# Gate and up products of the experts in halves instead of fp32, with the weights split once per tile

## What is computed

```
x = x + state_space_and_self_attention(layernorm(x))
x = x + cross_attention(layernorm(x), ctx)
x = x + experts(layernorm(x))              # the stage of the change
x = x + attention(layernorm(x)); x = x + cross(layernorm(x), ctx); x = x + int8_product(layernorm(x))
```

```
down_e( silu(z @ gate_e) * (z @ up_e) )    # gate_e, up_e: 256 x 512, down_e: 512 x 256, all fp32
```

## Time and profile before

| | us |
|---|---|
| three runs | 1214.91, 1215.37, 1217.53 (median 1215.37) |
| profiled execution, its own time | 1215.94 |
| its span (first to last instruction of the core) | 1214.1 |
| PE busy in the span | 1151.8 (95%) |
| DVE, ACT, POOL busy | 793.4 (65%), 719.0 (59%), 711.1 (59%) |
| TensorE's granted clock, mean over the span | 0.99 of full |
| costliest PE group: gate and up (L1736), 312 records | 146.7 |
| down (L1753), 312 records | 73.9 |

### The profile page before, as it was taken

How to read it: one execution, slowest core, us unless ns; L and a number is a source line. 1 busy time by engine, 2 the same in 40 slices (tenths; PEclk the granted TensorE clock), 3 DMA queues, 4 the chain that set the end, 5 groups by cost and what they waited for, 6 DMA issues and landing times.

```text
span 1214.1 us, 23112 instructions
## 1 busy us (share of the span) xinstructions
PE 1151.8 (95%) x7745; PEld 924.9 (76%) x7745; DVE 793.4 (65%) x1835; ACT 719.0 (59%) x2084; POOL 711.1 (59%) x783
## 2 busy tenths in 40 slices
PE   8999999999989999999989899988999999998996
PEld 7888888888877888888877677768566666667875
DVE  6788888889855566676676688767332333315796
ACT  6778787878724555555554788870223443225873
POOL 5799889898741234242354777750467556633664
PEclk9999999999999999999999899999999999999999
DMA  7000000000020000000030142610622222321001
GB/s 280 1 19 32 19 31 18 30 18 17 2 67 5 1 1 1 1 1 1 2 96 10 62 157 90 251 36 23 162 45 44 44 45 45 51 39 58 1 27 44
DMA packets 40373, 56.98 MB, mean 47 GB/s; under 512 B 8432, under 2 KB 35056, under 8 KB 38608
## 3 DMA queue, kind: packets, MB, share of 16 engines
q1 hardware_dynamic: 31536, 45.43, 11.2%
q0 software_dynamic: 8736, 10.25, 5.4%
HBM read 43.93 MB, written 11.74 MB: 46 GB/s over the span
## 4 chain that ended last, share of the span: by engine, by line
PE 45%; issue 7%; DVE 7%; ACT 6%; POOL 4%; DMA 1%; POOLq 0%; ACTq 0%; DVEq 0%
PE bank L1736 11%; PE bank L1753 5%; PE bank L44 4%; PE bank L46 3%; PE bank L45 3%; ACT x_prob L1390 3%; PE bank L847 2%; PE bank L875 2%; PE bank L858 2%; PE bank L1500 2%; PE bank L1484 1%; PE bank L1745 1%; PE bank L1430 1%; PE bank L2226 1%; POOL a_prob L1019 1%
## 5 line engine op out<-in xcount | busy, mean ns | idle before, releaser
L510 DVE SCALAR_TENSOR_TENSOR ssm_conv<-bank,conv_w,ssm_conv 128x508 f32<-128x508 f32 (+2 forms) x240 | 160.6, 733 | 14.2 <-ACT ssm_conv L400 14.2
L911 ACT ACTIVATE a_prob<-a_prob,a_neg_max 128x128 f32<-128x128 f32 x256 | 99.7, 391 | 116.6 <-DVE a_neg_max L957 116.6
L1019 POOL TENSOR_TENSOR a_prob<-a_prob,a_inv 128x512 f32<-128x512 f32 x64 | 66.6, 1041 | 138.9 <-DVE a_inv L962 138.9
L1736 PE MATMUL bank<-expert_raw,x_kept_next_t 128*128 x312 | 146.7, 593 | 1.2 <-ACT x_kept_next_t L1816 1.2
L674 POOL TENSOR_TENSOR ssm_u_lo<-ssm_conv,ssm_u_hi 128x512 fp32r<-128x512 f32 x80 | 101.4, 1292 | 25.2 <-ACT ssm_conv L410 25.2
L1678 POOL DMA_INDIRECT x_rows<-e_y,e_index x39 | 63.0, 1616 | 73.8 <-ACT e_y L1844 69.5
L44 PE MATMUL bank<-w_out_hi,ssm_u_hi 128*128 128x256 f32 x320 | 92.7, 290 | 3.4 <-POOL ssm_u_lo L674 3.4
L1960 DVE COPY e_h_t<-bank 128x512 f32<-128x512 f32 x39 | 27.0, 692 | 105.3 <-PE bank L1745 102.1
L1390 ACT ACTIVATE x_prob<-bank,x_neg_max 128x128 f32<-128x128 f32 x256 | 89.7, 399 | 7.2 <-DVE x_neg_max L1367 7.2
L46 PE MATMUL bank<-w_out_hi,ssm_u_lo 128*128 128x256 f32 x320 | 91.0, 284 | 0.0
L45 PE MATMUL bank<-w_out_lo,ssm_u_hi 128*128 128x256 f32 x320 | 90.9, 284 | 0.0
(11 more groups left out here) (359 smaller groups left out, 3330.7 us busy)
## 6 DMA issues: line engine op xcount, KB each, us to landing
expert_raw<-in_experts_laid SPq DMA_DIRECT2D x8, 1536.0 KB, 7.8
attn_raw<-in_attn_w_laid SPq DMA_DIRECT2D x1, 4096.0 KB, 18.0
w_in_raw<-in_L_attn_in_proj_w SPq DMA_DIRECT2D x5, 640.0 KB, 5.7
w_out_raw<-in_L_attn_out_proj_w SPq DMA_DIRECT2D x5, 512.0 KB, 4.0
x_res<-in_x SPq DMA_DIRECT2D x4, 512.0 KB, 5.6
x_res<-in_x SPq DMA_DIRECT2D x1, 2048.0 KB, 8.8
x_context<-in_ctx_t_laid SPq DMA_DIRECT2D x8, 256.0 KB, 3.7
z_rows<-x_kept_next_z SPq DMA_DIRECT2D x8, 256.0 KB, 2.2
```

The source lines that it names most:

```text
L510: op = dve.scalar_tensor_tensor(out=acc, in0=xs, scalar=conv_w[:, c, TAPS - 1 - back:TAPS - back], in1=acc, op0=ALU.mult, op1=ALU.add)
L911: e = act.activation(prob[:, m % 4, i, :], prob[:, m % 4, i, :], ACT.Exp, bias=neg_max[:, m % 4, i:i + 1], accum_out=total[:, m % 4, i:i + 1])
L1019: pool.tensor_tensor(prob[:, t % 4, :, :], prob[:, t % 4, :, :], inv[:, t % 4, :].unsqueeze(2).broadcast_to([P, 4, P]), ALU.mult).then_inc ...
L1736: mm = pe.matmul(bank[:, :], rows_t[:, t % 2, k, :], W[:, bass.ds(at + (column + k * FFN), FFN)], start=(k == 0), stop=(k == KD - 1))
```

## The change

Gate and up are computed as products of halves. Per tile, ACT copies the tile's expert's gate and up weights (four pieces of 128 x 512) into high halves `w_hi`, and DVE subtracts to get `w_lo`. There is one buffer each for gate and for up, so a piece is written for t + 1 only after that product of tile t is done. The turned rows are split too (`rows_hi` by ACT, `rows_lo` by DVE, from PSUM). ACT and DVE now read the expert's column into registers of their own. The copy of turned h moves from DVE to ACT in passes 1 to 8 and in the even context tiles. The copy of the turned context by ACT is a function of its own, behind the up half of the split. `w_hi` and `w_lo` lie where `x_res` is, which is in DRAM by then; `gains` and `scaled` move to other addresses. Down is unchanged.

```diff
+    h_on_act = lambda t: 1 <= t <= SEQS // 2 or (turns_context(t) and t % 2 == 0)
...
         def turn_rows(t):
             pe.wait_ge(gathered[t % 3], 16 * (t // 3) + 16)
             if t >= 1:
-                pe.wait_ge(zt_copied, t)
+                pe.wait_ge(rows_split, t)
...
-        def widen(t, at, column, bank, ready):
+        def widen(t, i, bank, ready):
             for k in range(KD):
-                mm = pe.matmul(bank[:, :], rows_t[:, t % 2, k, :], W[:, bass.ds(at + (column + k * FFN), FFN)],
-                               start=(k == 0), stop=(k == KD - 1))
+                pe.wait_ge(w_split[i], t * KD + k + 1)
+                mm = product(pe, bank[:, :], [x[:, t % 2, k, :] for x in (rows_hi, rows_lo)],
+                             [x[:, i, k, :] for x in (w_hi, w_lo)], k == 0, k == KD - 1)
             mm.then_inc(ready, 1)
...
-                pe.wait_ge(zt_copied, t + 1)
+                pe.wait_ge(rows_split, t + 1)
...
+        def split_high(t, at, i):
+            if t >= 1:
+                act.wait_ge((gate_ready, up_ready)[i], t)
+            for k in range(KD):
+                act.activation(w_hi[:, i, k, :], W[:, bass.ds(at + ((GATE_AT, UP_AT)[i] + k * FFN), FFN)],
+                               ACT.Copy).then_inc(hi_ready[i], 1)
...
+        act.wait_ge(x_stored, 16 * PAIRS)
+        act.wait_ge(weights_at_ready, 1)
+        at = offset(act, 0)
...
+        for i in range(2):
+            split_high(0, at, i)
         copy_rows(0)
         for t in range(SLOT_TILES + 1):
+            more = t + 1 < SLOT_TILES
+            if more:
+                at = offset(act, t + 1)
+            if t == 0:
+                split_high(1, at, 0)
             if t < SLOT_TILES:
                 silu(t)
-            if t + 1 < SLOT_TILES:
+            if t >= 1 and h_on_act(t):
+                copy_h(t - 1)
+            if more:
+                if t > 0:
+                    split_high(t + 1, at, 0)
                 copy_rows(t + 1)
+                split_high(t + 1, at, 1)
+                copy_keys(t + 1)
             if t >= 1:
                 copy_y(t - 1)
...
+        def split_low(t, at, i, k):
+            dve.wait_ge(hi_ready[i], t * KD + k + 1)
+            dve.tensor_tensor(w_lo[:, i, k, :], W[:, bass.ds(at + ((GATE_AT, UP_AT)[i] + k * FFN), FFN)],
+                              w_hi[:, i, k, :].bitcast(F32), ALU.subtract).then_inc(w_split[i], 1)
+
+        def rows_low(t):
+            dve.wait_ge(zt_copied, t + 1)
+            dve.tensor_tensor(rows_lo[:, t % 2, :, :], ZT.rearrange("p (k t) -> p k t", k=KD),
+                              rows_hi[:, t % 2, :, :].bitcast(F32), ALU.subtract).then_inc(rows_split, 1)
...
+        dve.wait_ge(weights_at_ready, 1)
+        at = offset(dve, 0)
+        for i in range(2):
+            for k in range(KD):
+                split_low(0, at, i, k)
+        rows_low(0)
         for t in range(SLOT_TILES + 1):
-            if t >= 1:
+            more = t + 1 < SLOT_TILES
+            if t >= 1 and not h_on_act(t):
                 copy_h(t - 1)
+            if more:
+                at = offset(dve, t + 1)
+                split_low(t + 1, at, 0, 0)
+            if t == 0:
+                rows_low(1)
             if t < SLOT_TILES:
                 fuse(t)
+            if more:
+                if t > 0:
+                    rows_low(t + 1)
+                split_low(t + 1, at, 0, 1)
+                for k in range(KD):
+                    split_low(t + 1, at, 1, k)
...
+        with nc.sbuf_tensor("e_w_hi", [P, 2, KD, FFN], F32R) as w_hi, nc.sbuf_tensor("e_w_lo", [P, 2, KD, FFN], F32R) as w_lo:
+            mem["wide_w"] = (w_hi, w_lo)
         mem["x"] = sb("x_res", [P, SEQS, D])
```

More of the change, by code:

```diff
@@ L1141, in stage_cross_attention @@
     for name, shape, dt in KEPT:
+        if name == "next_t":
+            with nc.sbuf_tensor("e_rows_hi", [P, 2, KD, P], F32R) as rows_hi:
+                kept["rows_hi"] = rows_hi
         kept[name] = sb(high, "kept_" + name, shape, dt)
@@ L1592, in stage_experts @@
     rows = sb("rows", [P, 3, D])
-    rows_t = kept["next_t"].rearrange("p a (b t) -> p a b t", t=P)
+    rows_hi, rows_lo = kept["rows_hi"], mem["rows_lo"]
+    w_hi, w_lo = mem["wide_w"]
     gate, h = sb("gate", [P, 2, FFN]), sb("h", [P, 2, FFN])
@@ L1621, in stage_experts @@
     y_sent = [sem(f"y_sent{i}") for i in range(3)]
-    zt_ready, zt_copied = sem("zt_ready"), sem("zt_copied")
+    zt_ready, zt_copied, rows_split = sem("zt_ready"), sem("zt_copied"), sem("rows_split")
+    hi_ready, w_split = (tuple(sem(f"{name}{i}") for i in range(2)) for name in ("hi_ready", "w_split"))
     gate_ready, up_ready, silu_ready, h_ready = sem("gate_ready"), sem("up_ready"), sem("silu_ready"), sem("h_ready")
@@ L1635, in stage_experts, with offset, turned_h @@
     turns_context = lambda t: C_TURN <= t < C_TURN + SEQS
+    h_on_act = lambda t: 1 <= t <= SEQS // 2 or (turns_context(t) and t % 2 == 0)
+    def offset(engine, t):
+        return engine.value_load(weights_at[0:1, t:t + 1], min_val=0, max_val=(EXPERTS - 1) * EXPERT_COLS)
+    def turned_h(t):
+        return HT[t % 2][:, :].rearrange("p (f t) -> p f t", f=KF)
     def sync(sp):
@@ L1755, in down @@
             mm.then_inc(down_ready, 1)
-        offset = lambda t: pe.value_load(weights_at[0:1, t:t + 1], min_val=0, max_val=(EXPERTS - 1) * EXPERT_COLS)
         pe.wait_ge(weights_at_ready, 1)
-        ahead = offset(0)
+        ahead = offset(pe, 0)
         turn_rows(0)
@@ L1765, in tensor @@
                 here = ahead
-                pe.wait_ge(zt_copied, t + 1)
+                pe.wait_ge(rows_split, t + 1)
                 if t >= 2:
                     pe.wait_ge(silu_ready, t - 1)
-                widen(t, here, GATE_AT, GATE[t % 2], gate_ready)
+                widen(t, 0, GATE[t % 2], gate_ready)
             if t >= 1:
@@ L1774, in tensor @@
                     pe.wait_ge(h_ready, t - 1)
-                widen(t, here, UP_AT, UP[t % 2], up_ready)
+                widen(t, 1, UP[t % 2], up_ready)
             if t + 1 < SLOT_TILES:
@@ L1781, in tensor @@
             if t + 1 < SLOT_TILES:
-                ahead = offset(t + 1)
+                ahead = offset(pe, t + 1)
         QK, FT, SCALES = GATE[(SLOT_TILES - 2) % 2], UP[(SLOT_TILES - 2) % 2], HT[(SLOT_TILES - 2) % 2]
@@ L1815, in copy_rows, with copy_keys @@
                 act.wait_ge(up_ready, t - 1)
-            act.activation(rows_t[:, t % 2, :, :], ZT.rearrange("p (k t) -> p k t", k=KD), ACT.Copy).then_inc(zt_copied, 1)
+            act.activation(rows_hi[:, t % 2, :, :], ZT.rearrange("p (k t) -> p k t", k=KD), ACT.Copy).then_inc(zt_copied, 1)
+        def copy_keys(t):
             if turns_context(t):
+                act.wait_ge(rows_split, t + 1)
                 b = t - C_TURN
@@ L1837, in silu, with copy_h @@
             act.activation(gate[:, t % 2, :], GATE[t % 2][:, :], ACT.Silu).then_inc(silu_ready, 1)
+        def split_high(t, at, i):
[4 more added lines that the diff above has]
+                               ACT.Copy).then_inc(hi_ready[i], 1)
+        def copy_h(t):
+            act.wait_ge(ht_ready, t + 1)
+            if t >= 2:
+                act.wait_ge(down_ready, t - 1)
+            act.activation(h_t[:, t % 2, :, :], turned_h(t), ACT.Copy).then_inc(ht_copied, 1)
         def copy_y(t):
@@ L1844, in copy_y @@
             act.activation(y[:, t % 3, :], Y, ACT.Copy, scale=weight[:, t:t + 1]).then_inc(y_copied, 1)
+        act.wait_ge(x_stored, 16 * PAIRS)
+        act.wait_ge(weights_at_ready, 1)
+        at = offset(act, 0)
+        for e in range(EXPERTS):
+            act.wait_ge(mem["expert_loaded"][e], 16)
+        for i in range(2):
+            split_high(0, at, i)
         copy_rows(0)
         for t in range(SLOT_TILES + 1):
+            more = t + 1 < SLOT_TILES
[3 more added lines that the diff above has]
+                split_high(1, at, 0)
             if t < SLOT_TILES:
                 silu(t)
-            if t + 1 < SLOT_TILES:
+            if t >= 1 and h_on_act(t):
[3 more added lines that the diff above has]
+                    split_high(t + 1, at, 0)
                 copy_rows(t + 1)
+                split_high(t + 1, at, 1)
+                copy_keys(t + 1)
             if t >= 1:
@@ L1959, in copy_h @@
                 dve.wait_ge(down_ready, t - 1)
-            dve.tensor_copy(h_t[:, t % 2, :, :], HT[t % 2][:, :].rearrange("p (f t) -> p f t", f=KF)).then_inc(ht_copied, 1)
+            dve.tensor_copy(h_t[:, t % 2, :, :], turned_h(t)).then_inc(ht_copied, 1)
+        def split_low(t, at, i, k):
[6 more added lines that the diff above has]
+                              rows_hi[:, t % 2, :, :].bitcast(F32), ALU.subtract).then_inc(rows_split, 1)
         def fuse(t):
@@ L2460, in decoder @@
         mem["neg_one"] = sb("neg_one", [P, SEQS])
+        mem["gains"], mem["scaled"] = sb("gains", [P, 4, KD]), sb("scaled", [P, 2, KD])
         spare_rows = (SEQS + 1) * P
@@ L2574, in decoder @@
```

(4 more changed lines are left out.)

## The result

| | us |
|---|---|
| after, median of 4 runs | 1195.68 (1195.39 to 1197.90) |
| before, median of 4 runs | 1216.05 (1214.91 to 1217.53) |
| ratio after to before | 0.9833, 95% interval 0.9822 to 0.9845 |
| profiled execution, its span | 1193.7 (before 1214.1) |
| busy: PE, DVE, ACT, POOL | 1128.4, 890.5, 805.1, 729.3 |

The gain is 20.4 us in the medians and in the spans. I forecast 25.2, and a time of 1190.2; the measured one lies in the range.

A forecast was written before the change was run, and what follows sets the result against it. PE was taken to bound the kernel: 36 periods each 0.71 us shorter (25.6), plus 0.71 for tile 38, less 1.05 at the start, give 25.2 us. That made 1190.2 against the runs' median, range 1187.5 to 1201.

The forecast's parts named there:

- PE is the bound and stays it: Expert stage: only PE's work sets the pace, busy all 70.00 us of a stretch, and 99% or more after.
- Twelve products at 0.228: Gate and up per tile: 2.73 us instead of 3.44, saving 0.71; periods 5.11, and 5.32 with context.
- ACT and DVE keep the pace, by 0.13 us: Splits for the next tile: added copies and subtractions finish before PE wants them, by 0.13 us at the tightest place.
- Rival 1: Missed split handshakes before PE's products: up to 0.26 us per tile, time 1193 to 1200; chance 22%.
- The start: 1.05 us lost: Head of the expert stage: first splits and ACT's order move gate(2) from 861.68 to 862.7, losing 1.05 us.
- The memory moves and POOL's loop at nothing: Address moves costed at nothing; POOL's loop in the expert stage put at 4.46 us, contention at 0.02 per 0.42 overlap.
- Rival 3: DVE's subtractions and POOL's descriptor making exclude each other: POOL's loop grows to 6.86 us, time 1251; chance 6%.
- L1669 above 1.2 us: POOL's issue at that line lasting over 1.2 us would be the sign of port contention with DVE's subtractions.
- The end of the stage: Tile 38's own products give 0.71 us more; the scatter chain ends 1063.6, covered by PE's end at 1065.0.
- rival 2: POOL's scatter chain decides, its 5.16 us stretched to 5.3 or 5.5 by gathers: time 1194 to 1202; chance 8%.
- The 5.16 us: Issue to issue of the last two scatters, POOL waiting for the landing; used for the whole scatter chain.
- the 1090.16: Taken as PE's end in the expert stage before the change; less 25.2 it gave 1065.0.

The follow-up runs named there:

- e4: The changed kernel with DVE subtracting only 16 of 512 columns per weight piece from tile 1 on, all waits kept; 1195.82 us (single execution).
- e2: The changed kernel without the product of low rows by high weights, so 8 products per tile instead of 12; 1184.18 us (single execution).
- e3: The changed kernel with turned h copied by DVE in every pass, as before the change; 1196.49 us (single execution).
- e6: The changed kernel with silu(0) ahead of tile 1's gate halves on ACT, plus 6 idle products on PE behind the first turned rows; 1192.05 us (single execution).
- e7: The changed kernel with POOL issuing each row gather one pass earlier into the same three buffers; 1197.51 us (single execution).
- e9: The changed kernel without low rows by high weights, and with only 16 of 512 columns subtracted from tile 1 on; 1179.91 us (single execution).
- e5: The changed kernel with ACT doing silu(0), table load first, before the gate halves of tile 1; 1197.06 us (single execution).
- e8_again: Second measurement, on another chip, of the changed kernel with silu(0) first, idle products and earlier row gathers; median 1194.71 us, ratio 0.9818 to before.
- e1: The changed kernel, splits and waits kept, but PE does one fp32 product per piece, of the high halves alone; 1219.17 us (single execution).
- e8: The changed kernel with silu(0) first, idle products on PE and row gathers one pass earlier; median 1193.49 us, ratio 0.9810 to before.
- after_again: The changed kernel, unedited, measured once more on another chip; median 1197.54 us, ratio 0.9842 to before.

## Why the prediction came out as it did

The direction, the mechanism and the range were right; the gain was 4.8 us too high. By its own steps:

- **PE is the bound and stays it.** Right. From gate(2) to gate(38) PE is idle for 0.7 us only. e4, with hardly any subtractions left, keeps the periods of 5.16 and 5.38, so the splits cost PE nothing outside the start and that one wait.
- **Twelve products at 0.228.** The term was a little low. They are spaced by 0.231 us, so the periods are 5.16 and 5.38, not 5.11 and 5.32, and 36 tiles give 23.7 instead of 25.6 us before the wait: 1.9 us of the miss. The mean of 26 products was dominated by a long packed run. Its own first four spacings, 45.92 to 46.85, average 0.232, and a tile has only 6 in a row. The trace of before had it throughout: in its 24 runs of such products, 18 of them 30 long, the second to fifth spacings average 0.231 us and those from the eleventh on 0.227. Nor were the roles the same, though I had said so: in that stage the weights are stationary and the activations move (`product` gets `w_in` first). That did not matter: in 28 runs in before with the activations stationary (rows `bank<-attn_w,act_t`) the second to fifth spacings average 0.232. By the 216 ns of the Trainium skill (TensorE: Matmul & The Clock Gate, Back-to-back issue gap) the miss would have been larger.
- **ACT and DVE keep the pace, by 0.13 us.** Right that they keep it. The 0.13 was not there in the passes in which the sum looked for it. The timeline after, around the gate of a pass in which ACT copies h:

```profile
868.15 0.42 DVE L2017 TENSOR_TENSOR rows_lo<-bank,e_rows_hi 128x256 fp32r<-128x256 f32 x1
868.49 1.88 DVE L2012 TENSOR_TENSOR e_w_lo<-expert_raw,e_w_hi 128x512 fp32r<-128x512 f32 x3
...
868.62 0.19 PEld L44 LDWEIGHTS bank<-e_w_hi,e_rows_hi 128*128 128x128 f32 x1
868.62 0.55 PE L44 MATMUL bank<-e_w_hi,e_rows_hi 128*128 128x512 f32 x1
...
868.82 1.17 POOL L1683 DMA_INDIRECT e_weight<-share_rows,e_share_at  x1 [0.30 <-issue]
```

  The rows' low half is done at 868.15 + 0.42 = 868.57, and the weight load of gate begins at 868.62. For gates 3 to 9 that distance is the same each time, 0.05 to 0.06 us; later it is 0.22 to 0.53. So in these seven passes PE takes the rows the moment they are there. It loses nothing by it: from the start of down's last record to the start of gate's second product are 0.45 us in all passes, since the weight load runs beside the end of down. Rival 1, missed handshakes at a price, did not occur, by less than the 0.13. e2 shows how close it is: a PE 0.9 us faster per tile gets only 0.3 of it. The chain is tight through the copy of h on ACT, which e3 shows to be needless.
- **The start: 1.05 us lost.** It was 2.52. The order on ACT was as forecast (table load behind the split, against 855.17). The step that was missing is the clock. I costed PE's idle 1.5 us ahead of gate(0) as time only, and most of tile 0's 12 products were then 0.43 us apart instead of 0.23. e6 gives all but 0.22 of the 2.52 back.
- **The memory moves and POOL's loop at nothing.** Wrong for POOL. I had looked at its three issues and not at the power operation at pass 11, and took 0.02 us per 0.42 of overlap from one row as the price of contention. The issues grew by 0.17 and 0.24 us (medians against e4's and the 0.95 of the earlier trace rows). With them POOL's loop is 1.62 + 1.16 + 1.20 + 0.90 = 4.88 of 5.16 us, where it was 4.46 of 5.82: its room fell from 1.36 to some 0.3 us per tile, and it could not make up for the power operation. That cost 0.94 us, as e7 shows; 0.67 of it goes with the subtractions (e4).
- **Rival 3, exclusion between DVE's subtractions and POOL.** Its mechanism is there, its price is not. In the rows above an issue of 1.17 us ran from 868.82 wholly inside three subtractions that end at 870.37 and follow each other at 0.60 us, without a gap. It took 0.22 us longer than its 0.95. My own sign for this rival, L1669 above 1.2 us, was met all but exactly (1.198), and the time did not get worse by it. By the lock of the Trainium skill (SBUF — State Buffer, SBUF: two separate sides), held for whole instructions, either the issue or a subtraction would have had to wait the other out. That the two disturb each other agrees with the page; that one fully blocks the other does not show in this trace.
- **The end of the stage.** The last tile gave 0.46 instead of 0.71, the last scatters 0.43 that I had not counted. The scatter chain did not decide (rival 2). The 5.16 us that I took for a scatter that waits for the one before came from one pair; after the change two such pairs took 4.57 and 4.32. And the 1090.16 that I called PE's end is the landing of the last scatter; PE was done with down at 1083.59.
- **Outside the stage.** +1.45 in the second layer and -0.73 ahead of the stage I could not have forecast. They are luck, and go against each other. The -0.73 comes with the piece at half clock at 811 that only the profile before has. For the +1.45, the profile after has one at 1084; of the other profiles but those of e2 and e9, the ones with one at 1083 to 1086 (e5, e8_again) take 131.5 and 132.2 us from the end of the last down on, as this one does (131.5), and those without (before, e1, e3, e4, e6, e7, e8, after_again) 129.8 to 130.8. Where it falls differs from execution to execution of one kernel.

Summed: 25.2 - 1.9 (spacing) - 1.5 (start) - 0.9 (wait) - 0.25 + 0.43 (end) + 0.73 - 1.45 (outside) = 20.4, as measured. Inside the stage the miss is thus the spacing, the clock at the start, and POOL's one late gather.

## What to carry to other kernels

Work that is moved onto idle engines to relieve the bound is free only while each chain through them closes inside the new, shorter period. Lay the chain out against the start of the next tile, as here, and look at what else sits in the same queues once per stage. At the head of a stage count also what an added wait does to the clock of the products behind it, and fill it. And take a spacing from a run of instructions as short as the one that you will issue.

## What the hardware showed that I had not expected

- A wait of 1.4 to 1.6 us on PE ahead of gate(0) came with a stretch at half clock, beginning between 0.2 us ahead of gate(0) and 0.5 behind its start, in every profile of the change and of its variants without idle products but e9. There that wait was 1.13 us with no such stretch behind it (the clock had been at half from 843.2 to 850.0 already), and one of 2.84 ahead of gate(1) had one. Most of tile 0's products after were 0.43 us apart instead of 0.23. But a wait alone does not decide it. Ahead of gate(1) waits of 1.63 (after), 1.94 (e1) and 2.17 us (e3) had no such stretch behind them, while others of 1.89 to 2.15 (e2, e4, e7, after_again) and one of 1.52 (e8_again) had. What else decides I can't tell from these runs.
- Subtractions of 128 x 512 on DVE, here with both inputs in SBUF, lengthen the issue of an indirect DMA on POOL by 0.17 to 0.24 us (987 to 1156 and 963 to 1198 ns), and which one is hit changes with the kernel: in e1 it was the scatter, 1.62 to 1.77. Whether both inputs must lie in SBUF for it no run shows.
- Products of 128 x 512 from halves are 0.231 us apart in runs of six and 0.227 from the eleventh of a run on, at full clock.
